# The loop body that every engine runs, 32 groups long in place of 16

## Time and profile before

| | us |
|---|---|
| median of 3 runs | 8270.77 |
| lowest and highest of them | 8262.04, 8276.08 |
| the profiled execution | 8265.89 |
| its span, first to last instruction | 8264.0 |

### The profile page before, as it was taken

One profiled execution on the slowest core, in us unless ns is written; L12 is line 12 of the kernel. 1 busy time (PEld: TensorE's weight loads), 2 busy tenths in 40 slices (PEclk: granted clock), 3 DMA queues, 4 the chain that ended last, 5 costly groups with the idle time before them and its releaser, 6 DMA issues. The chain is left out here.

```text
span 8264.0 us, 254328 instructions
## 1 busy us (share of the span) xinstructions
PE 7871.5 (95%) x77810; PEld 5168.3 (63%) x77810; DVE 6299.5 (76%) x26070; ACT 6214.3 (75%) x10999; POOL 4684.1 (57%) x7940
## 2 busy tenths in 40 slices
PE   6899999999999999999999999999999999999997
PEld 5666666666666666666666666666666666666663
DVE  4477778777777877877777787787777778777773
ACT  2377777777777777777777777777777777777774
POOL 1355556566565565655556555565555565565553
PEclk9999999999999999999999999999999999999999
DMA  0001111111111111111111111111111111111111
GB/s 24 4 26 36 36 35 34 37 36 33 37 36 32 36 37 33 35 37 36 33 36 37 32 36 37 33 36 37 36 33 37 34 34 37 37 32 36 36 34 42
DMA packets 216033, 281.61 MB, mean 34 GB/s; under 512 B 30371, under 2 KB 214216, under 8 KB 214344
## 3 DMA queue, kind: packets, MB, share of 16 engines
q1 hardware_dynamic: 214600, 264.20, 11.3%
HBM read 235.04 MB, written 28.90 MB: 32 GB/s over the span
## 5 line engine op out<-in xcount | busy, mean ns | idle before, releaser
L1281 ACT ACTIVATE ht<-ps,be 128x392 f32<-128x392 f32 x4096 | 2253.6, 584 | 346.0 <-PE ps L707 170.6
L707 PE MATMUL ps<-ht,we 128*64 128x392 f32 x8192 | 1584.4, 508 | 39.4 <-ACT ht L1281 25.0
L697 PE MATMUL ps<-xs,we_hi 128*128 128x392 f16 x4096 | 1370.6, 335 | 166.9 <-ACT ht L1281 166.8
L697 PE MATMUL ps<-xs,we_lo 128*128 128x392 f16 x4096 | 1349.2, 329 | 0.0
L1088 POOL TENSOR_TENSOR sc<-sc,mx 113x392 f32<-113x392 f32 x1024 | 896.0, 884 | 707.4 <-DVE mx L872 707.2
L707 PEld LDWEIGHTS ps<-ht,we 128*64 128x64 f32 x8192 | 498.9, 136 | 714.0 <-issue 550.8
L1174 ACT ACTIVATE pt<-ps 98x392 f32<-98x392 f32 x1024 | 506.9, 495 | 512.3 <-PE ps L557 487.1
L697 PEld LDWEIGHTS ps<-xs,we_hi 128*128 128x128 f16 x4096 | 410.2, 100 | 685.0 <-issue 384.6
L1074 POOL TENSOR_TENSOR rs<-ve,cs 98x4 f32<-98x4 f32 x768 | 781.2, 1017 | 21.4
L1105 POOL TENSOR_TENSOR kvsd<-kvsd,cs 98x128 f32<-98x128 f32 x256 | 101.9, 398 | 1218.0 <-ACT kvsd L1247 1218.0
L1067 POOL TENSOR_TENSOR ve<-mv,cs 98x4 f32<-98x4 f32 x768 | 154.2, 201 | 981.8 <-DVE mv L830 981.7
(11 more groups left out here) (185 smaller groups left out, 18858.7 us busy)
## 6 DMA issues: line engine op xcount, KB each, us to landing
gb<-gates SPq DMA_DIRECT2D x1024, 196.0 KB, 3.7
xg<-in_x SPq DMA_DIRECT2D x256, 98.0 KB
out_y<-yo SPq DMA_DIRECT2D x256, 98.0 KB
gates<-gtt SPq DMA_DIRECT2D x256, 12.2 KB
bias<-in_rel SPq DMA_DIRECT2D x1, 1200.5 KB
bias<-in_w SPq DMA_DIRECT2D x2, 512.0 KB
gb<-in_amask SPq DMA_DIRECT2D x2, 300.1 KB
we<-in_w SPq DMA_DIRECT2D x1, 512.0 KB
```

The lines of the kernel that those rows point to most:

```text
L697: last = pe.matmul(pH[b % 2][:, 0:GTOK], we1[half][:, 128 * b:128 * (b + 1)], xs[:, g.j % 2, :], start=(half == 0), stop=(half == 1))
L707: last = pe.matmul(pY[C * e:C * (e + 1), 0:GTOK], we2[:, b, :], ht[:, b % 8, :], start=(h == 0), stop=(h == 1), skip_group_check=True)
L1281: act.activation(ht[:, b % 8, :], pH[b % 2][:, 0:GTOK], ACT.Gelu, bias=be1[:, b:b + 1], scale=1.0 / WSCALE).then_inc(S["h_ready"], 1)
```

## The change

A constant `LOOP = 32` takes the place of `BODY` in `program` and in `Group.image`. The loop's body is 32 iterations, so that the 256 groups are 8 bodies: 1 in the head, 6 turns of the loop, 1 in the tail. The head ends at the same iteration as before; the tail begins at 224 in place of 240. `BODY` stays 16 where it is the number of groups that the buffers hold, and every `-BODY` wait is as it was.

```
+LOOP = 32
...
     def image(self, d=0):
-        return 2 * self.at + (self.c + d) // (BODY // 2)
+        return LOOP // (BODY // 2) * self.at + (self.c + d) // (BODY // 2)
...
-            bodies = TOTAL // BODY
-            head = min(2, bodies)
+            bodies = TOTAL // LOOP
+            head = min(1, bodies)
             tail = max(bodies - 1, head)
-            for n in range(-LEAD, BODY * head):
+            for n in range(-LEAD, LOOP * head):
                 iteration(0, n, n, n)
             if tail > head:
                 count = eng.alloc_register()
-                eng.reg_mov(count, head * BODY - 1)
+                eng.reg_mov(count, head * LOOP - 1)
                 with eng.Fori(head, tail) as i:
-                    for c in range(BODY):
+                    for c in range(LOOP):
                         eng.reg_add(count, count, 1)
-                        iteration(i, eng.snap(count), c, BODY * head + c)
-            for n in range(BODY * tail, TOTAL + LAG):
+                        iteration(i, eng.snap(count), c, LOOP * head + c)
+            for n in range(LOOP * tail, TOTAL + LAG):
                 iteration(0, n, n, n)
```

## The result

| | before | after |
|---|---|---|
| median, us | 8271.6 (6 runs, 8262.04 to 8277.77) | 8238.68 (6 runs, 8236.1 to 8242.82) |
| ratio, 95% interval | | 0.9961 [0.9951, 0.9971] |
| the profiled execution, us | 8265.89 | 8242.82 |
| its span, us | 8264.0 | 8241.0 |

The change makes the kernel 0.4% faster, 33 us by the medians and 23 us by the two profiled executions. 8248.5 was forecast, a gain of 20; the measured time lies 0.7 us inside the lower end of the range of 8238 to 8260, and under the 8240 where the forecast's own case ended.

A forecast was written before the change was run, and what follows sets the result against it. TensorE, busy 95% of the span, was taken to bound the kernel. Seven fewer jumps back (-21.0) and more straight code (+0.7) sum to -20.3 us, giving 8248.5 us, range 8238 to 8260.

The forecast's parts named there:

- the forecast's own case: Fewer jumps back make the whole kernel faster: 8248.5 us, own range 8240 to 8257, chance 0.83.
- The edges: Jumps back to the loop body's start: 5 in place of 12, seven saved at 3.0 us each, -21.0 us.
- the fetch of the body's beginning: At each jump back, engines wait for the body's first instructions, which aren't at hand; TensorE idles some 2 us.
- The free pace: Loop stretches of 8 groups without a jump back: expected to stay at 245.3 us, no gain.
- the 16 straight groups: Iterations 224 to 239 move from loop to tail, where straight code is slower: +0.4 to +1.0, taken as +0.7 us.
- The dips that stay as many: TensorE's low-clock periods keep their own beat, so only idling at jumps back is saved: 14.0 us, 8254.7; chance 0.08.
- The untaken branch's price: A loop jump costs only 83 ns, pauses come from something else every 16 groups: 8268.8 us; chance 0.05.
- Register work in a long body: 32 iterations' counter copies overload TensorE's sequencer in the loop, making it slower: 8295 us; chance 0.04.
- took the work for hidden: In the loop, TensorE's 1.2 us a group of register instructions is covered by queued matmuls, since straight code isn't faster.
- signs of being wrong: Loop stretches without a jump back over 245.4 us, a jump back over 3.7 us, or half clock away from jumps.
- The 987 us between branches: Expected distance between the loop's branches in the changed kernel, in place of 494 us.
- whose pause it is: At a jump back, TensorE's some 2 us stop is its own sequencer's; other engines have the same gap at theirs.

The follow-up runs named there:

- loop64: Loop body of 64 groups (`LOOP = 64` in the changed kernel), one jump back; 8235.6 us (5 runs), ratio 0.996 against the kernel before.
- body16_six: Kernel before with its body of 16 groups but 9 bodies in the head, so 6 turns and five jumps back; 8253.0 us, ratio 0.998.
- one_turn: Changed kernel with a loop body of 192 groups run once, 32 groups each in head and tail, waits still from registers; 8229.0 us, ratio 0.9949.
- straight: Changed kernel with `LOOP = 256`, so nothing loops and no register work remains; 8242.4 us (6 runs), ratio 0.9967.

## Why the prediction was right, and where its size was off

**The edges: right, and the bulk of it.** 12 x 3.03 = 36.4 us before and 5 x 2.81 = 14.0 after: -22.3 against the forecast's -21.0, and within its -18 to -27. Number and length of the branches are as written, the idling behind each is the same, and on top of it the clock takes nothing, 1.4 or 2.9 us. The low clock stands behind 34 of 48 edges before and 7 of 15 after; that the mean edge came out a little cheaper after is no more than that, and was luck. The five edges together cost 17.3, 10.9 and 14.0 us in the three profiles, enough for the 7 us over which single runs of the changed kernel scatter. The twelve of before differ by 2.4 us only, so the 16 us of its single runs are not explained by them. What the pause itself is, which the prediction reads as the fetch of the body's beginning, no run tests; TensorE's branch lasts 3.4 to 3.9 us in both kernels and in `loop64`, so bodies of 16, 32 and 64 pay alike; one of 4.5 us stands in the profile of `body16_six`.

**The free pace: put at nothing, gained 2.** The stretches without an edge or a stray dip have a mean of 245.38 us in the four profiles before, 245.28 in the three after, since some in the longer body reach the 245.0 that `one_turn` keeps up (`body16_six` does too, with its short body, so the length alone isn't what gives it). Over 19 stretches of the loop that is -2. With it stands the +0.3 that the 16 straight groups cost (245.5, 245.6 and 245.8 where 245.4, 245.3 and 245.8 stood), forecast at +0.7, and +0.2 for stray dips (5 in four profiles before, 4 in three after). So -22.3 - 1.9 + 0.3 + 0.2 = -23.7, and the table gives 7376.7 - 7400.5 = -23.8.

**The end: no term of mine, -2.** From group 241 on -2.1 in the mean, with a spread of 4 us in each kernel. By the windows above it is how much of the last 365 us runs at the low clock; whether the mean differs at all can't be told from seven profiles. Setup differs by half a us the other way.

Together the profiles give -25 us, where 20.3 was forecast. The medians give 33 and 34. The remaining 8 us stay open. Because of them the measured time lies at the range's lower end and not in its middle, and it is inside only thanks to the 2 us by which the range reaches below the forecast's own 8240. Three of the four profiled executions of before (8265.3 to 8266.2 us) lie under all its medians (8268.3 to 8271.6), the fourth (8268.5) at the lowest; on the chip of the last two another execution of before took 8282.4. Three of after lie about its own medians (8234.9, 8242.8, 8245.5 against 8237.2 and 8238.7). Either the profiled ones of before were on the cheap side by chance, or an unprofiled edge costs somewhat more; no run here tells these apart, but at 4.5 us for every edge `straight` and the body of 64 would have been faster than they are.

**The rivals.** The dips that stay as many (8254.7): refuted, with 9, 9, 11 and 10 of them before group 241 in the profiles before and 4, 1 and 6 in those after. Even the nine of them that follow no edge at once aren't free of the edges: each lies 238 to 242 us behind a branch, in the changed kernel too, whose branches are 985 us apart; of the kernels without an edge `one_turn` has none before group 241, and `straight` one, at 4588.5 us. The untaken branch's price (no change): refuted by the ratio. The Trainium skill (Advanced Engine Details and Errata, Control Flow Timing) gives 108 ns for a compare-and-branch; in this trace the 83 ns of the branch not taken are near it, and the 3644 of those taken are far from it. Register work in a long body (8295): refuted by `loop64` and `one_turn`; waits from registers are, if anything, the faster kind here. The prediction took the work for hidden because straight code has none of it and isn't faster; that was a weaker reason than it seemed, since straight code has more wait instructions in its place (the last section has their number).

**What the prediction listed as signs of being wrong.** Two of its three turned up in part. Single edges cost more than 3.7 us (two of 4.9), though not the mean; and low clock away from an edge came once, never and three times, where before it came once or twice. The 987 us between branches was a wrong sum: a body of 32 holds one edge, 4 x 245.3 + 3.0 is 984.2, and the five distances have a mean of 985.0.

**The step that was half right** is whose pause it is. It didn't enter the sum, since all engines lose the same edges, but anyone who had acted on it, and had freed TensorE alone of its loop, would have kept 1.8 of 3.0 us an edge.

## What to carry to other kernels

In a loop that each engine runs for itself, count the jumps back and read their price as a difference of the pace with and without one; it is the pause and then what the clock takes for the pause. Freeing one engine of the jump doesn't remove it, as the pauses of the others come through their semaphores. Fewer jumps by a longer body were worth having here, but writing everything straight is not the end of that road: 192 groups in one turn (8229.0 us) beat no loop at all (8242.4).

## What the runs showed that I had not expected

- Two waits of 0.5 to 0.75 and 1.3 us left TensorE's clock at 2.4 GHz at all 12 edges; one of 1.85 to 2.4 us was followed by 1.2 GHz in most cases, 11 of 12 in one kernel and 8 of 12 in another.
- The same last 2254 matmuls took from 360 to 371 us in three kernels, with more of the clock's low stretches in the longer ones and no other difference found in the traces; that is a third of what the change itself is worth by the medians.
- Straight code on ScalarE alone makes 8 groups 0.3 us longer (245.6 against 245.3), though it has less to execute in all. What it has more of is wait instructions, 12 more a group. The lines of all 256 groups, 208 of them in the loop in the first kernel (before) and none in the second (`straight`):

```profile
L316 ACTq EVENT_SEMAPHORE  x4375: 17/17/38, 83.1 to 8250.4; - x199
```

```profile
L317 ACTq EVENT_SEMAPHORE  x6871: 17/17/38, 83.0 to 8227.4; - x197
```

Whether these are the cause is not shown. The loss appears in TensorE's one longer wait for the expert activation in each group, 5.3 us in 8 groups of `straight` against 4.8 in the loop.
